# Filler matrix products on TensorE at both edges of the two deep calls and in the time stage, twelve sublayers in one launch

## What is computed

```python
def _L3_ffn_ref(x, ...):                      # "deep"
    for i in range(DEPTH):                    # 6
        x = attn_layer(shift_tokens(x), Wqkv[i], q_scale[i], k_scale[i], Wo[i]) + x
        x = ffn_layer(shift_tokens(x), ln_g[i], ln_b[i], W1[i], b1[i], W2[i], b2[i]) + x
    return x
...
def _L3_attn_ref(x, ...):                     # "time"
    k, v = einsum(xk, Wk), einsum(xv, Wv)
    sr = sigmoid(einsum(xr, Wr))
    rwkv = sr * _wkv(time_decay, time_first, k, v)    # a scan along the tokens
    return einsum(rwkv, Wo)
...
x = x + 0.5 * _L3_ffn_ref(_layernorm(x), ...)
x = x + _L3_attn_ref(_layernorm(x), ...)
x = x + 0.5 * _L3_ffn_ref(_layernorm(x), ...)
```

## Time and profile before

| | us |
|---|---|
| three runs, median (lowest to highest) | 4470.68 (4459.03 to 4475.77) |
| the profiled execution | 4482.51 |
| its span, first to last instruction | 4480.8 |
| PE busy | 4247.5 (95%) |
| DVE, ACT, POOL busy | 3201.0, 2674.7, 2127.7 |
| mean granted clock of TensorE | 0.956 |

### The profile page before, as it was taken

The page is one execution under the profiler, slowest core; times in us unless marked ns, Lnnn a source line. Parts: engine busy times, 40 slices in busy tenths (PEclk is TensorE's granted clock), DMA queues, the critical chain, the costliest instruction groups (busy, mean ns, idle before and its releaser), DMA issues.

```text
span 4480.8 us, 148099 instructions
## 1 busy us (share of the span) xinstructions
PE 4247.5 (95%) x66444; PEld 2382.4 (53%) x66444; DVE 3201.0 (71%) x4171; ACT 2674.7 (60%) x3161; POOL 2127.7 (47%) x1151
## 2 busy tenths in 40 slices
PE   7998999867999999999999995799999999999998
PEld 4543433334555555555555552455555555555554
DVE  3564666465777777777777766687787787787784
ACT  1451355323776776776776761576776776776774
POOL 0110000013666666666666640666665665666662
PEclk8898899978999999999999997899999999999998
DMA  2000000001111112111111111111211212121111
GB/s 85 1 2 1 1 1 1 1 0 40 33 29 53 39 28 59 33 53 34 33 53 34 33 28 50 24 33 32 56 33 31 56 33 55 32 58 29 33 33 29
DMA packets 78739, 144.92 MB, mean 32 GB/s; under 512 B 18656, under 2 KB 25120, under 8 KB 76576
## 3 DMA queue, kind: packets, MB, share of 16 engines
q1 hardware_dynamic: 78112, 135.45, 11.7%
HBM read 39.97 MB, written 1.05 MB: 9 GB/s over the span
## 4 chain that ended last, share of the span: by engine, by line
PE 80%; POOL 7%; issue 6%; DVE 5%; ACT 2%; DMA 0%; SPq 0%; POOLq 0%; DVEq 0%; ACTq 0%
PE psum L1321 13%; PE psum L1373 7%; PE psum L1346 7%; PE psum L1334 6%; PE psum L1290 5%; PE psum L681 5%; PE psum L1392 5%; PE psum L1304 4%; PE psum L1422 3%; PE psum L713 3%; PE psum L1438 3%; PE psum L1432 3%; PE psum L735 3%; PE psum L1387 3%; POOL arena L1753 3%
## 5 line engine op out<-in xcount | busy, mean ns | idle before, releaser
L1753 POOL TENSOR_TENSOR arena<-arena 128x1024 f32<-128x1024 f32 x384 | 722.3, 1902 | 883.8 <-ACT arena L1501 883.8
L1747 POOL TENSOR_TENSOR arena<-arena 128x1024 f32<-128x1024 f32 x384 | 907.3, 2363 | 246.3 <-DVE arena L1622 246.3
L1618 DVE TENSOR_TENSOR arena<-psum,arena 128x1024 f32<-128x1024 f32 x384 | 467.6, 1218 | 619.5 <-ACT arena L1494 619.0
L1494 ACT ACTIVATE arena<-psum 128x1024 f32<-128x1024 f32 x384 | 392.0, 1021 | 288.9 <-PE psum L1321 288.9
L1373 PEld LDWEIGHTS psum<-arena 64*64 64x64 f32 x24576 | 396.4, 135 | 211.5 <-issue 211.4
L1507 ACT ACTIVATE arena<-psum 128x1024 f32<-128x1024 f32 x384 | 390.5, 1017 | 194.5 <-PE psum L1334 194.5
L1622 DVE TENSOR_TENSOR arena<-psum,arena 128x1024 f32<-128x1024 f32 x384 | 466.2, 1214 | 0.0
L1629 DVE TENSOR_REDUCE h_pair<-arena 128x16 f32<-128x1024 f32 x384 | 464.1, 1209 | 0.0
L1373 PE MATMUL psum<-arena 64*64 64x32 f32 x24576 | 438.8, 221 | 4.9 <-DVE arena L1596 4.7
L1334 PE MATMUL psum<-w_ident,arena 128*128 128x128 f32 x3072 | 416.4, 279 | 23.0 <-POOL arena L1753 14.7
L1334 PEld LDWEIGHTS psum<-w_ident,arena 128*128 128x128 f32 x3072 | 338.8, 141 | 161.0 <-POOL arena L1753 91.5
(11 more groups left out here) (266 smaller groups left out, 6997.6 us busy)
## 6 DMA issues: line engine op xcount, KB each, us to landing
arena<-arena SPq DMA_DIRECT2D x672, 128.0 KB, 2.4
deep_wqkv<-in_deep_wqkv SPq DMA_DIRECT2D x6, 1536.0 KB, 6.9
arena<-in_deep_wqkv SPq DMA_DIRECT2D x6, 1536.0 KB, 6.7
arena<-arena SPq DMA_DIRECT2D x96, 64.0 KB, 2.0
deep_wo<-in_deep_wo SPq DMA_DIRECT2D x6, 512.0 KB, 7.4
arena<-in_deep_wo SPq DMA_DIRECT2D x6, 512.0 KB, 7.4
deep_w<-in_deep_w SPq DMA_DIRECT2D x6, 341.0 KB, 7.6
arena<-in_deep_w SPq DMA_DIRECT2D x6, 341.0 KB, 7.5
```

Of the source, the lines that this page charges most:

```text
L1494: nc.scalar.activation(qk_sq[:, HALVES[half], :], qk_half, ACT.Square).then_inc(de.deep_qk_squared, 1)
L1618: nc.vector.tensor_tensor(turned[:, hs, :].rearrange("p h (a e) -> p h a e", a=2), swapped, sin, ALU.mult).then_inc(de.deep_rope_parts, 1)
L1747: nc.gpsimd.tensor_tensor(roped[a % 2][:, hs, :], roped[a % 2][:, hs, :], turned[:, hs, :], ALU.add).then_inc(de.deep_summed, 1)
L1753: nc.gpsimd.tensor_tensor(roped[a % 2][:, hs, :], roped[a % 2][:, hs, :], over(h_inv[a % 2][:, hs], [P, LHEADS, LD]), ALU.mult).then_inc(d ...
```

## The change

A new helper `busy_pe(n, to)` issues n products of the bf16 identity with 512 columns of the bf16 mask (64 columns, read eight times), each with its own start and stop, into a PSUM bank that nobody reads in that state. They wait for nothing and signal nothing. There are 216 of them: in each deep call 14 behind the spread and ahead of `deep_pe`, 4 times 12 in the steps 0 and 1, one block behind each `qk_pe`, and 31 in the steps of the last unit (8, 6, 6, 7 and 4); and 30 in the time stage, behind the third output projection and ahead of the wait of the fourth. No other instruction is added, taken away or moved.

```diff
+        def busy_pe(n, to):
+
+            for _ in range(n):
+                nc.tensor.matmul(to, identb[:, :], maskb[:, 1, :].rearrange("p (o c) -> p o c", o=1).broadcast_to([P, 8, 2 * WIN]),
+                                 start=True, stop=True)
...
                 if kind == "o":
+                    if b == NB - 1:
+                        busy_pe(30, bank(VAR_BANK))
                     pe.wait_ge(tm.tm_y_ready, b + 1)
...
                 if s < ALL:
                     qk_pe(pe, c, s, 0)
+                if s < 2:
+                    busy_pe(12, bank(6))
...
+                last = n - 2 == UNITS - 1
                 if t == 0 and ending:
+                    if last:
+                        busy_pe(6, bank(0))
                     var_pe(pe, c, n - 2)
+                    if last:
+                        busy_pe(6, bank(0))
                 if t == 1 and ending:
+                    if last:
+                        busy_pe(7, bank(0))
                     gate_pe(pe, c, n - 2, 0)
...
                 if s < ALL:
                     qk_pe(pe, c, s, 1)
+                if s < 2:
+                    busy_pe(12, bank(6))
...
                 if t == 3 and begun:
+                    if n == UNITS:
+                        busy_pe(8, bank(2))
                     mean_pe(pe, c, n - 1)
...
                 if t == 1 and ending:
+                    if last:
+                        busy_pe(4, bank(0))
                     gate_pe(pe, c, n - 2, 2)
                     a_pe(pe, c, n - 2, 0)
...
                     for b in range(NB):
                         quad_spread_pe(pe, q, b)
+                    busy_pe(14, bank(0))
                     deep_pe(pe, call)
```

## The result

| | before | after |
|---|---|---|
| median of 13 runs each (lowest to highest) | 4470.68 us (4450.96 to 4485.82) | 4434.06 us (4425.81 to 4457.87) |
| ratio, 95% interval | | 0.9939 (0.9921 to 0.9956) |
| the profiled execution | 4482.51 us | 4448.09 us |
| its span | 4480.8 us | 4446.4 us |
| mean granted clock | 0.956 | 0.968 |

What follows compares the result with a forecast made beforehand. TensorE was taken as the bound, its products at deep starts and ends slowed by low clock; 19.4 - 0.5 + 6.8 + 1.5 = 27.2 us won, from the 4470.7 us median to 4443.5 us, range 4434 to 4462 us.

Steps and rivals of the forecast that it cites:

- The filler's price: One filler product on TensorE takes 0.21 us at full clock, 0.43 us at half, its weight load hidden.
- The first rival: A filler costs 0.43 us at full clock, so blocks outlast their waits: 8 us slower, 4479 us; chance 0.07.
- The starts: Starts of both deep calls: projection halves and query transposes at full clock win 19.4 us together, 0.5 us taken off.
- Block four: Fourth block of twelve at a deep start, ahead of the key transposes: 3.6 us where 3.50 were free, 0.1 us lost.
- All five halves: Projection halves on the path at a deep start: 18.27 us falls to 9.40 us at 1.88 each, 8.9 us won.
- the lead: The 14 fillers ahead of a deep call's first half: 3.0 us at full clock within 3.74 us of idleness.
- The ends: End of each deep call: mean, variance, spread and gates at full clock win 3.4 us, 6.8 us for both calls.
- The time stage: 30 fillers ahead of the last output projection: projection and means shorter, some 0.4 us late, net 1.5 us won.
- the second rival: Fillers, being constants, do not bring the clock up: nothing won, 38 us lost, 4509 us; chance 0.06.
- The third rival: Shifted clock falls: added, 5 to 15 us lost, about 4454 us, chance 0.22; spared, 4435 us, chance 0.06.
- The sign of being wrong that was named: Blocks ending after the next product's semaphore, first 14 at clock 0.50, or won time returning as TensorE idle time later.
- The fourth rival: Transposes do not lift the clock, so the 14 start at half clock: 4.4 us less won, 4448 us; chance 0.03.

Runs made afterwards that it cites:

- no_lead: Changed kernel without the 14 fillers ahead of the first projection half; ran once, first half to first scores 26.26 and 26.11 us (24.36 in the changed kernel).
- one_column: Changed kernel with all 216 fillers kept in place but each streaming one column in place of 512; ratio to before 0.9996 (0.9979 to 1.0014).
- kick: Changed kernel plus 24 fillers, two ahead of each half step 1 to 6 of the mqa stage's attention; 4459.05 us in its one run.
- wider: `further` plus filler pairs in the mqa and rope attentions and fillers in waits of untouched stages; median 4425.0 us, ratio to before 0.9908.
- further: Changed kernel without the four fillers among the gates, with 6, 6 and 7 in three other waits; median 4444.2 us, ratio to before 0.9934.
- wider_less: `wider` without its 24 fillers in the mqa attention; median 4430.91 us, ratio to before 0.9912 (0.9884 to 0.9941).
- starts_only: Changed kernel with only the fillers at the two deep calls' starts, none at the ends or in the time stage; ratio to before 0.9970.

## Why the prediction was right, step by step

The stretches that carry fillers gave 26.6 us where 27.2 were summed, and by the steps that were named: the mechanism is the one that was predicted. The ratio, 0.9939, is the forecast's (4443.5 of 4470.68); with an interval of 0.9921 to 0.9956, that it agrees to the fourth place is luck. So is that the median of after, 4434.06 us, falls just inside the range: it lies 9.4 us under the forecast, and under its own range of 4436 to 4449 us.

- **The filler's price**, taken as 0.21 us between bounds of 0.21 and 0.43: 12 in 2.75 us. The load, 0.10 us each, is hidden. The first rival falls, and with it the rule of the Trainium skill (TensorE: Matmul & The Clock Gate, Part 3, The mechanism) by which loads of the same row group do not overlap with products in flight (the section excepts loads into a background weight buffer): these loads all have the same rows, and the trace does not agree.
- **The starts**, 19.4 us less 0.5: 18.8 less 0.7 us. The ramp came out at 24.36 us where 24 was named. Block four cost about what was counted. Two terms are mis-sized. All five halves were counted at 1.88 us; three of them took 1.98 or 1.99, 0.3 us in each call. And the lead cost 0.2 us more than was taken off: it ran partly at half clock (4.33 us for 14 in the first call, 4.02 in the second). The prediction took the lead as the condition of the whole win, and that was wrong: `no_lead` shows that it pays only 1.4 us a call, since without it the clock came up in the first half or in the first block of twelve.
- **The ends**, 3.4 us each: 3.37 us. The waits left 0.69, 0.22 and twice under 0.2 us, as the sums said.
- **The time stage**, 1.5 us net: 1.7 us. The last output projection was not 0.4 us late: it came 9.13 us behind the one before it (2758.33 to 2767.46 us), as it did before with 2.07 us of product and 7.06 us of wait.
- **Fillers of constants lift the clock** (against the second rival): 1.00 from 1040 to 1070 us. `one_column` is that rival made true, without its cost, and gives 0.9996.
- **The third rival** (falls of the clock added or spared) went the other way right behind the ramps, by 2.3 us. The sign of being wrong that was named, a deep call's middle that changes, did come in the first call, 6.2 us longer. The clock fell in it near the end (0.83 on the mean from 2640 to 2680 us, 0.91 in before), and once TensorE stood idle for 1.62 us. Nothing ties it to the fillers: the second call was 2.7 us shorter, and in the other twelve traces this way takes 1505.0 to 1510.5 us, with fillers at the start or without.
- **The fourth rival** (transposes do not lift the clock) had the 14 begin at half clock in each call, and so they did: the clock came up 2.3 us into them in the first call and 1.7 us in the second, behind transposes that ran at 0.50 throughout (3.93 and 3.94 us for 16). What that cost is 0.7 us in all and not 4.4. That transposes never lift the clock is not borne out: in the second call of before they were all that TensorE did from 2794.53 to 2798.28 us, and the clock was 0.50 from 2795 to 2797 us and 1.00 from 2798 us on.
- **What the median has beyond the sum.** 26.6 us lie in the edited stretches, and the ratio makes 27 us of it; but the medians differ by 36.6 us and the profiled pair by 34.4. The step that falls short is not a term but the anchor: the prediction set one profiled execution 11.8 us over the median of three and took that distance as fixed, and the third rival priced a fall of the clock at some 2 us. The largest, in the mqa attention, part the ten traces by 19 us, and the start of the first deep call by 27. Whether the median's further 10 us are such chance in 13 runs of each kernel no run tells; ahead of the first deep call, where the profiled pair's excess arose, the two kernels do the same, so the fillers cannot be its cause there.

## What to carry to other kernels

Where TensorE waits for others and its own products stand whole between the waits, read those products' length against the same record elsewhere at granted clock 1.00: the difference is the most that fillers can win there. Size each block so that it ends just inside its wait (one filler here is 0.21 us, what a block has over its wait is paid whole, and a wait half full may not keep the clock up), and put none where TensorE is the bound: in the mqa attention 24 of them cost 7.6 us. Sum the stretches that were edited, and treat what the total has beyond that sum as the clock's chance until a run shows otherwise.

## What the runs showed of the hardware that was not expected

- The same instructions, with hardly a gap, ran at granted clock 0.50 until 160 us in one execution and at 0.97 from 139 us on in another (mqa attention). Each us at half clock cost 0.40 us there; this alone parts executions of the same code by up to 19 us.
- Pairs of full fillers among small products left the clock at 0.50 in `kick` (41.00 of 41.00 us busy) and stood beside a clock that came up after 17.1 us in `wider`; while a block of 14 ran at the same place it came up (one trace each).
- Near the end of the first deep call of after TensorE stands idle once for 1.62 us, released by nothing that the profile shows, within products that follow each other without a gap in before; `further`, `wider_less` and `starts_only` have 1.23, 1.22 and 0.88 us of the kind in their second calls. No experiment was made on it.

```profile
2669.27 0.50 PE L1381 MATMUL psum<-arena 64*64 64x32 f32 x11 [1.62 <-issue]
```
